# Two small attentions of a perceiver kernel: a second pair of score banks, and a new order of tiles on TensorE and VectorE

## The reference

```python
# first: 16 heads of 32; query t sees keys 0..t of the context's first 64 rows
scores = jnp.einsum('bhqd,bhqwd->bhqw', q, k_win)
scores = jnp.where(mask, -jnp.inf, scores)
m = jnp.max(scores, axis=-1, keepdims=True)
e = jnp.exp(scores - m)
probs = e / jnp.sum(e, axis=-1, keepdims=True)
ctx = jnp.einsum('bhqw,bhqwd->bhqd', probs, v_win)
x = x + ctx @ o_w.T + o_b
...
# second: 16 heads of 64, no mask, 64 keys
scores = jnp.einsum('bqhd,bkhd->bhqk', q, k) * SCALE
attn = jax.nn.softmax(scores, axis=-1)
out = jnp.einsum('bhqk,bkhd->bqhd', attn, v)
x = x + out @ Wo + bo
```

## Time and profile before

| | us |
|---|---|
| median of 3 runs | 1509.92 (1509.21 to 1511.82) |
| the profiled execution's own time | 1511.36 |
| its span | 1509.3 |
| TensorE busy | 1416.2 |
| VectorE busy | 728.9 |
| ScalarE busy | 509.0 |

### The profile page before, as it was taken

The page is one execution under the profiler, slowest core; times in us unless marked ns, Lnnn a source line. Parts: engine busy times, 40 slices in busy tenths (PEclk is TensorE's granted clock), DMA queues, the critical chain, the costliest instruction groups (busy, mean ns, idle before and its releaser), DMA issues. The chain is left out here.

```text
span 1509.3 us, 26710 instructions
## 1 busy us (share of the span) xinstructions
PE 1416.2 (94%) x11200; PEld 1058.5 (70%) x11200; DVE 728.9 (48%) x1337; ACT 509.0 (34%) x839; POOL 368.4 (24%) x228
## 2 busy tenths in 40 slices
PE   7889987899998999999999999999999997997995
PEld 6858774545457788888887887887878865434783
DVE  6669779789463323322323233223232233676933
ACT  3434222333121153433432534234325343613702
POOL 7120100000131331312231313132313111306911
PEclk9779979999989999999999999999999999999997
DMA  5412200102034121111110211111102016003000
GB/s 205 168 57 77 78 1 1 77 0 84 0 111 128 52 64 33 52 38 58 40 55 28 64 33 52 38 57 41 56 26 64 23 53 257 1 0 133 0 1 28
DMA packets 49573, 88.01 MB, mean 58 GB/s; under 512 B 28584, under 2 KB 41136, under 8 KB 46128
## 3 DMA queue, kind: packets, MB, share of 16 engines
q1 hardware_dynamic: 49456, 86.32, 16.5%
HBM read 76.61 MB, written 9.70 MB: 57 GB/s over the span
## 5 line engine op out<-in xcount | busy, mean ns | idle before, releaser
L1345 POOL TENSOR_TENSOR ctx_hi<-ctx_raw,one 128x1536 fp32r<-128x1536 f32 (+1 forms) x32 | 91.5, 2858 | 567.4 <-DMA ctx_raw<-in_ctx 363.9
L1543 ACT COPY ET<-PS 128x512 f32<-128x512 f32 (+1 forms) x224 | 129.4, 585 | 276.8 <-PE PS L1447 201.4
L1646 DVE TENSOR_SCALAR_CACHE_REDUCE E<-PS 128x384 f32<-128x384 f32 (+1 forms) x256 | 131.8, 571 | 180.6 <-PE PS L1424 180.0
L1615 DVE TENSOR_TENSOR V<-PS,vbias 128x512 f32<-128x512 f32 (+1 forms) x104 | 71.7, 690 | 192.9 <-PE PS L1391 192.8
L1391 PE MATMUL PS<-ctx_raw_r,wk_hi 128*128 128x384 f32 (+1 forms) x512 | 128.2, 355 | 0.0
L1391 PE MATMUL PS<-wv_lo,ctx_hi 128*128 128x512 f32 (+1 forms) x416 | 127.6, 406 | 0.0
L1550 ACT ACTIVATE E<-E,peak 128x1601 f32<-128x1601 f32 x64 | 103.5, 1622 | 66.9 <-DVE peak L1651 66.9
L1447 PE MATMUL PS<-ident,E 128*128 128x128 f32 (+1 forms) x832 | 122.9, 273 | 0.0
L1391 PE MATMUL PS<-ctx_hi,wk_hi 128*128 128x384 f32 (+1 forms) x512 | 120.6, 357 | 1.5 <-POOL ctx_raw_r L1348 1.5
L1391 PE MATMUL PS<-wv_hi,ctx_hi 128*128 128x512 f32 (+1 forms) x416 | 120.4, 411 | 0.8 <-issue 0.8
L1348 POOL TENSOR_TENSOR ctx_raw_r<-ctx_raw,ctx_hi 128x1536 fp32r<-128x1536 f32 (+1 forms) x32 | 116.9, 3653 | 2.5
(11 more groups left out here) (320 smaller groups left out, 2225.4 us busy)
## 6 DMA issues: line engine op xcount, KB each, us to landing
ctx_raw<-in_ctx SPq DMA_DIRECT2D x24, 768.0 KB, 4.4
ctx_raw<-in_ctx_first SPq DMA_DIRECT2D x8, 900.0 KB, 4.5
rel_scr<-rel_out SPq DMA_DIRECT2D x8, 640.0 KB, 3.6
fwk<-in_fwk SPq DMA_DIRECT2D x1, 4096.0 KB, 12.4
fwv<-in_fwv SPq DMA_DIRECT2D x1, 4096.0 KB, 12.4
corr<-rel_scr SPq DMA_DIRECT2D x64, 48.0 KB
p_scr<-E SPq DMA_DIRECT2D x16, 192.0 KB, 2.3
near<-p_scr SPq DMA_DIRECT2D x64, 48.0 KB
```

Of the source, the lines that this page charges most:

```text
L1345: nc.gpsimd.tensor_tensor(ctx_hi[r][:, :, 0:n], ctx_raw[r][:, :, 0:n], one[:].unsqueeze(1).broadcast_to([P, KC, n]), ALU.mult).then_inc(S[ ...
L1543: nc.scalar.copy(ET[0:n, j % ET_RING, :], src[0:n, :]).then_inc(S["et_out"], 1)
L1615: v.tensor_tensor(V[0:rows, at % V_RING, :], bank(4 + NUMBER[unit] % 2)[0:rows, :], vbias[0:rows, :], ALU.add).then_inc(S["v_out"], 1)
L1646: v.tensor_scalar(E[:, p, k0:k0 + n], bank(r)[:, 0:n], 1.0, None, ALU.mult, ALU.max, accum_out=tops[:, p, c:c + 1]).then_inc(S["s_out"], 1)
```

## The change

Tile t's scores go to banks 0 and 1 for an even t and 2 and 3 for an odd t, the transposes to banks 6 and 7, and the projection of tile t to bank t. scores(t) waits for the banks' last reader two tiles back. Project(t) waits that the scores in its bank have been read. The orders on TensorE and on VectorE are written out anew, one for both attentions. In the first attention values(0) also waits until ScalarE has built BQ of all tiles, since that reads banks 5 to 7.

```diff
+        score_bank = lambda t: 2 * (t % 2)
+        y_bank = lambda t: t
...
-                if t >= 1:
-                    pe.wait_ge(s_free if mask else shifted, t)
+                if t >= 2:
+                    pe.wait_ge(s_free if mask else shifted, t - 1)
...
                 if t >= 1:
                     pe.wait_ge(pt_out, t)
+                elif queries:
+                    queries.tensor(pe, NT - 1)
...
             def project(t):
                 pe.wait_ge(o_out, t + 1)
-                if t >= 2:
-                    pe.wait_ge(x_done, t - 1)
-                linear_to_tokens(nc, bank(6 + t % 2), oT, t, s.w[w_out], 0, D, groups).then_inc(y_ps, 1)
+                pe.wait_ge(s_free if mask else shifted, 3 + t // 2)
+                linear_to_tokens(nc, bank(y_bank(t)), oT, t, s.w[w_out], 0, D, groups).then_inc(y_ps, 1)
...
-            if mask:
-                scores(0), scores(1), values(0), scores(2), context(0), values(1), scores(3), context(1)
-                values(2), project(0), context(2), values(3), project(1), context(3), project(2), project(3)
-            else:
-                scores(0)
-                for t in range(NT):
-                    if t + 1 < NT:
-                        scores(t + 1)
-                    if t >= 1:
-                        project(t - 1)
-                    values(t)
-                    context(t)
-                project(NT - 1)
+            scores(0), scores(1), values(0), scores(2), context(0), values(1), scores(3), context(1), project(0)
+            values(2), context(2), project(1), values(3), project(2), context(3), project(3)
...
-            soften(0)
-            for t in range(NT):
-                weigh(t)
-                if t + 1 < NT:
-                    soften(t + 1)
-                other(2)
-                if t >= 1 and not mask:
-                    residual(t - 1)
+            soften(0), soften(1), weigh(0), other(2), soften(2), weigh(1), other(2), soften(3), weigh(2), other(2)
+            residual(0), weigh(3), other(2), residual(1)
             if beside:
                 beside.finish(dve, ch)
-            if mask:
-                for t in range(NT - 1):
-                    residual(t)
+            residual(2)
```

More of the change, by code:

```diff
@@ L360, in scores @@
                     queries.tensor(pe, t)
-                if t >= 1:
-                    pe.wait_ge(s_free if mask else shifted, t)
+                if t >= 2:
+                    pe.wait_ge(s_free if mask else shifted, t - 1)
                 for b in range(2):
                     for hp in range(HP):
-                        last = nc.tensor.matmul(bank(b)[:, hp * SQ:(hp + 1) * SQ], s.BQ[:, hp, 2 * t + b, :],
+                        last = nc.tensor.matmul(bank(score_bank(t) + b)[:, hp * SQ:(hp + 1) * SQ], s.BQ[:, hp, 2 * t + b, :],
                                                 s.KT[:, hp // pairs_in_group, (2 * t + b) * SQ:(2 * t + b + 1) * SQ],
@@ L373, in values @@
                     pe.wait_ge(pt_out, t)
+                elif queries:
+                    queries.tensor(pe, NT - 1)
                 for hp in range(HP):
-                    last = nc.tensor.transpose(bank(2 + hp // 4)[:, hp % 4 * P:(hp % 4 + 1) * P],
+                    last = nc.tensor.transpose(bank(6 + hp // 4)[:, hp % 4 * P:(hp % 4 + 1) * P],
                                                pr[:, t % 2, hp, :, :].rearrange("p b k -> p (b k)"), s.ident[:])
@@ L419, in residual @@
                 dve.wait_ge(y_ps, t + 1)
-                nc.vector.tensor_tensor(s.X[:, t, :], bank(6 + t % 2), s.X[:, t, :], ALU.add).then_inc(x_done, 1)
+                nc.vector.tensor_tensor(s.X[:, t, :], bank(y_bank(t)), s.X[:, t, :], ALU.add).then_inc(x_done, 1)
                 dve.wait_ge(x_done, t + 1)
@@ L427, in soften @@
                 dve.wait_ge(s_ps, t + 1)
-                both = s.PS[:, 0:2, :].rearrange("p b (h k) -> p b h k", k=SQ)
+                both = s.PS[:, score_bank(t):score_bank(t) + 2, :].rearrange("p b (h k) -> p b h k", k=SQ)
                 if mask:
@@ L489, in _ @@
                 nc.scalar.copy(pT[:, t % 2].rearrange("p h n -> p (h n)"),
-                               s.PS[:, 2:4, :].rearrange("p b n -> p (b n)")).then_inc(pt_out, 1)
+                               s.PS[:, 6:8, :].rearrange("p b n -> p (b n)")).then_inc(pt_out, 1)
                 act.wait_ge(o_ps, t + 1)
```

## The result

The changed kernel takes 1520.64 us (median of 8 runs, 1520.11 to 1530.28), against 1509.74 for the kernel before (8 runs beside it): ratio 1.0074, with a 95% interval of 1.0061 to 1.0087. So it is 10.9 us slower, where the forecast was 11.6 and a median of 1521.5. Its profiled execution took 1520.18 us, with a span of 1518.2, 8.9 more than before.

The account below looks back on a forecast made before the run. TensorE was taken to bound the first attention, with TensorE and VectorE close in the second. A loss of 11.6 us in the first plus 0 in the second gave a median of 1521.5 us, range 1513.5 to 1528.

Parts of the forecast that it names:

- Values(0) waits for soften(1) and weigh(0): First attention: values(0) starts at 70.8 in place of 65.37, 5.4 us later, with TensorE idle for 6.5 us.
- values(0) before 66: First attention: a sign that the prediction is wrong, values(0) coming before 66 us where about 70.8 was forecast.
- The two rounds: First attention, values(0) to values(2): 31.2 us at half clock or 22.8 at full clock, taken as the middle, 27.0.
- rival A: Gaps keep TensorE at 1.2 GHz through both rounds: first attention +19.3 us, second 0, whole 1529; chance 0.12.
- From values(2) to the end: End of the first attention: 20.3 us in place of 23.5, with project(0) hidden and two copies waited for.
- A together: First attention as a whole: ends at 118.1 in place of 106.45, 11.6 us slower, range +7.4 to +19.3.
- The wait for BQ ahead of values(0): First attention: values(0) also waits for BQ of all tiles, which ScalarE has built before; costs nothing.
- B: 0 forecast: Second attention as a whole: no change in its length, with bounds of -6.6 and +4 us.
- VectorE doesn't wait behind scores(2): Second attention: from there on VectorE doesn't wait, as values(1) and scores(3), 9.0 us, hide under a rounding piece of 9.7.
- The barrier carries all on: Behind both attentions: a barrier carries what an attention gains or loses to the end one for one.
- the ring: First attention: values(t), scores(t+2), soften(t+2), weigh(t+1), values(t+1) each wait for the one before; 15.6 us at half clock, 11.4 at full.
- Rival C: Both attentions: scores of t+1 run on TensorE while VectorE still reads tile t; 14.7 us less, 1495; chance 0.05.

Follow-up runs that it names:

- second profile: The changed kernel unchanged, run again for a second profile of it; 1529.76 us (one run).
- e6: Changed kernel plus three products that nobody reads in each of TensorE's two gaps in the first attention, ahead of values(0) and values(1); 1520.33 us.
- e9: Changed kernel plus products that nobody reads in the first attention, three ahead of values(0) and five ahead of values(1); 1522.43 us.
- e4: Changed kernel with scores(t+2) ahead of values(t) on TensorE in the first attention, VectorE's order still new; 1511.06 us.
- e3: Kernel before with VectorE's new order alone, banks and TensorE's order old; 1540.95 us, ratio 1.0205.
- e8: Changed kernel with TensorE's old orders, banks and VectorE's order still new; 1540.40 us, ratio 1.0203.
- e2: Kernel before with the new banks and their waits alone, both orders old; 1510.65 us, ratio 1.0003.
- e7: New banks with orders fitted: scores(t+2) ahead of values(t) in the first attention, VectorE reordered in the second; 1503.45 us, ratio 0.9951.
- e5: Changed kernel with VectorE's old order in the first attention alone; 1511.10 us, ratio 1.0007.

## Why the prediction was right, point by point

The sign and the cause were right. That the size came so near is partly luck: in A two terms that were off, by 5.2 and 4.1, nearly cancelled, and beside it 4.6 us less in B met 3.6 more in code that didn't change.

1. Values(0) waits for soften(1) and weigh(0). Right: a gap of 6.5 us was forecast, and 6.58 measured. Its time was wrong. I took scores(1) at half clock, as in the earlier trace rows, so that values(0) was 19.1 us behind the start (70.8 - 51.7). In the profile scores(0) and (1) ran at full clock, and it was 66.53 - 52.62 = 13.9; in the second one it was 18.1. This term was mis-sized by 5.2, or by 1.0 in the second profile. One of the signs of being wrong, values(0) before 66, nearly came true: it came at 66.53, and A had begun 0.9 later than in the kernel before. Against the kernel before, values(0) is only 0.2 us later from the start of A (13.9 and 13.7), for the idle 6.58 us are made up by scores at full clock; what A loses, it loses in the rounds.
2. The two rounds. The mechanism was right, but I took the middle of both levels, 27.0 us. Measured were 97.66 - 66.53 = 31.1 and, the second time, 30.6: both rounds at half clock, both times. That was rival A's half of the argument, and the mean clock of 0.75 that I reasoned from was a mean over other work. Off by 4.1 the other way. In the first profile 0.6 of it is project(0), which took 5.94 and ended after weigh(2), where I had it hidden. The Trainium skill's advice against idle gaps (TensorE: Matmul & The Clock Gate, "Why this matters for your kernels") agrees with these rounds, and with e6 and e9, where half clock stood behind the longer gaps. A gap isn't the whole of it: scores(0) to (2) of e4 ran 19.00 us without one at a mean granted clock of 0.55. The stretch from 200.5 to 213.5 us that the prediction leaned on is also weaker than it seemed, as scores(1), ahead of that gap, had taken 7.09 us, which is half clock, too.
3. From values(2) to the end 20.3 were forecast, with the open copies of 1.1 and 0.7; measured were 19.7, with rows of 1.10 and 0.68. Right.
4. A together: 66.4 forecast, 64.7 and 68.4 measured. The wait for BQ ahead of values(0) cost nothing, as forecast: no gap is put down to it.
5. B: 0 forecast, -4.6 measured in the first profile, +2.7 in the second, within the bounds of -6.6 and +4. The term that was off in the first profile is the half clock of scores(0) and (1): up to values(0) it took 12.6 and 16.9 us where I had 17.3, and VectorE's wait for scores(1) was 1.09 where I had 4.6. From there on, 66.1 us were forecast, and 66.1 and 69.2 measured. The statement that VectorE doesn't wait behind scores(2) held in the first profile (0.37 in all) and failed in the second, by the 3.43 for ScalarE. VectorE also ends B alone: project(3) was done at 265.9, and residual(3) began at 268.10 without a wait, where I had counted both engines to the same end.
6. The barrier carries all on, and nothing absorbs it. Right, but not to the us: in the first pair of profiles the rest of the program, whose code is the same, took 3.6 us more (0.9 ahead of A, 1.0 between, 1.7 behind). Over all profiles these three pieces were 51.4 to 52.9, 74.1 to 75.3 and 1243.0 to 1247.3 us. The last two show no order by kernel, but the first does: it is 52.3 to 52.9 in all six profiles whose A has the ring (changed twice, e3, e6, e8, e9) and 51.4 to 51.9 in the seven others, though the code ahead of A is the same. Why was not tried.

So the 8.9 us between the two spans are 9.9 in A, 4.6 less in B and 3.6 elsewhere. Rival C, that free banks let TensorE overlap, fell with e2: these banks alone are worth nothing that can be measured. It was right in one thing, which e4 and e7 show: the banks are worth something once the orders use them.

## What to carry to other kernels

A second buffer moves nothing by itself: look at what stands in the queue ahead of the step that it frees, on each in-order engine. A step put "a tile ahead" also pushes back the step that it passes; follow the ring (who waits for whom, once around) and price one round of it. Two orders written by hand on two engines have to be changed as a pair, and measured apart in each place that uses them, since here the same pair lost 10 to 15 us in one attention, while the other came out between 4.6 us shorter and 2.7 longer, by the clock. And where a step moves to another bank, look for the wait that comes with it.

## What was not expected of the hardware

The same instructions of scores(0) and (1), one behind the other without a gap, take 7.33 us or about 11.6 in the same program, by the clock that TensorE is granted (1.00 in the first profile and 0.54 in the second, over the bulk of them):

```profile
54.00:59.50 5.50, 5.50 (x52) 5.50 (x51) 3.01 (x3) 5.30 (x18) 3.39 (x3) 1.00 0.89 371
```

```profile
54.00:63.50 9.50, 9.50 (x50) 9.50 (x50) 3.67 (x3) 6.81 (x20) 3.09 (x3) 0.54 0.96 406
```

The runs of the changed kernel spread over 1520.1 to 1530.3 us, with a mean granted clock of 0.960 in the shortest and 0.948 in the longest, and those of e5 over 1506.8 to 1519.8, while the kernel before stays within 1508.2 to 1514.2 in all its runs. That the same steps make the whole of the spread is likely but shown by these two profiles alone. The program was the same in both; what decides it was not found.
